# Attention and SwiGLU on one core: the feed-forward's gate and up matmuls one group ahead of their own

## The reference

```python
xn = _layernorm(x, axis=-1)
# attention: 16 heads of 8 features, 4 key/value heads, rotary embedding on q and k
q = (xn @ Wq.T + bq); k = (xn @ Wk.T + bk); v = (xn @ Wv.T + bv)
probs = softmax(q @ k * HD ** -0.5)
attn = (probs @ v) @ Wo.T + bo
# feed-forward: hidden size 384, integer weights times 1/127
h = silu(xn @ wg.T) * (xn @ wu.T)
out = x + attn + h @ wd.T
```

## Time and profile before

| what | value |
|---|---|
| runs, median (lowest to highest) | 772.57 us (772.14 to 774.59), 3 runs |
| profiled execution, its own time | 775.68 us |
| its span | 773.9 us |
| TensorE busy | 722.5 us, 93% |
| VectorE busy | 692.7 us, 90% |
| ScalarE busy | 618.1 us, 80% |
| GpSimd busy | 223.5 us, 29% |
| mean granted clock of TensorE | 0.985 of full speed |

### The profile page before, as it was taken

How to read it: one execution, slowest core, us unless ns; L and a number is a source line. 1 busy time by engine, 2 the same in 40 slices (tenths; PEclk the granted TensorE clock), 3 DMA queues, 4 the chain that set the end, 5 groups by cost and what they waited for, 6 DMA issues and landing times.

```text
span 773.9 us, 13580 instructions
## 1 busy us (share of the span) xinstructions
PE 722.5 (93%) x4856; PEld 213.2 (28%) x4856; DVE 692.7 (90%) x1284; ACT 618.1 (80%) x1267; POOL 223.5 (29%) x364
## 2 busy tenths in 40 slices
PE   3598999999999999999999999999999999999996
PEld 1222222222222222222222222222222222222352
DVE  6787999999999999999999999999999999999731
ACT  1534979888888988888888989798888889898864
POOL 3408647373830302122030303021120303021110
PEclk9787999999999999999999999999999999999999
DMA  7511123131221101011111101011111111010021
GB/s 220 140 34 32 40 76 113 33 113 33 75 71 32 32 1 54 10 31 33 32 32 32 32 22 42 1 33 32 32 32 33 32 33 32 2 32 2 2 70 40
DMA packets 29323, 34.34 MB, mean 44 GB/s; under 512 B 5545, under 2 KB 20137, under 8 KB 29129
## 3 DMA queue, kind: packets, MB, share of 16 engines
q1 hardware_dynamic: 26472, 26.23, 12.2%
q0 software_dynamic: 1920, 5.12, 2.2%
q10 hardware_dynamic: 864, 2.15, 0.8%
HBM read 23.12 MB, written 9.96 MB: 43 GB/s over the span
## 4 chain that ended last, share of the span: by engine, by line
PE 74%; DVE 15%; ACT 5%; DMA 2%; issue 2%; SPq 1%; ACTq 0%; DVEq 0%
PE acc_ps L953 29%; PE banks L867 18%; DVE mx L719 13%; PE banks L884 11%; PE banks L958 8%; ACT probs L560 5%; PE banks L972 3%; PE banks L964 2%; DMA y_all<-in_x 1%; PE banks L837 1%; PE banks L989 1%; PE banks L843 1%; DMA k_rows<-part 1%; DVE y_all L766 1%; PE banks L980 0%
## 5 line engine op out<-in xcount | busy, mean ns | idle before, releaser
L719 DVE TENSOR_REDUCE mx<-banks 128x1 f32<-128x512 f32 x1024 | 637.9, 684 | 38.1 <-PE banks L867 36.0
L560 ACT ACTIVATE probs<-banks 128x512 f32<-128x512 f32 x1024 | 549.4, 604 | 101.9 <-PE banks L884 97.8
L884 PE MATMUL banks<-qc,kc 51*128 51x512 bf16 x1024 | 305.6, 384 | 15.6 <-ACT probs L560 10.6
L867 PE MATMUL banks<-ka,qa 48*128 48x512 bf16 x1024 | 300.6, 386 | 11.1 <-DVE mx L719 6.1
L953 PE MATMUL acc_ps<-probs,v_grp 128*32 128x512 f32 x2048 | 273.4, 606 | 0.0
L867 PEld LDWEIGHTS banks<-ka,qa 48*128 48x128 bf16 x1024 | 68.7, 94 | 303.4 <-DVE mx L719 235.5
L447 POOL TENSOR_TENSOR neg_max<-row_max,nought 128x16 bf16<-128x16 f32 x31 | 6.9, 222 | 295.4 <-DVE row_max L725 295.4
L884 PEld LDWEIGHTS banks<-qc,kc 51*128 51x128 bf16 x1024 | 66.0, 94 | 55.1 <-ACT probs L560 52.3
L958 PE MATMUL banks<-xn_T,w_ffn 128*128 128x256 f32 x192 | 67.5, 433 | 0.0
L953 PEld LDWEIGHTS acc_ps<-probs,v_grp 128*32 128x32 f32 x2048 | 40.4, 108 | 81.2 <-ACT probs L560 51.1
L491 POOL TENSOR_TENSOR gated<-gu 128x256 f32<-128x256 f32 x48 | 35.2, 733 | 53.4 <-ACT gu L617 53.4
(11 more groups left out here) (86 smaller groups left out, 310.1 us busy)
## 6 DMA issues: line engine op xcount, KB each, us to landing
qa<-q_rows SPq DMA_DIRECT2D x32, 192.0 KB, 3.4
qc<-q_rows SPq DMA_DIRECT2D x64, 96.0 KB, 2.7
q_rows<-part POOLq DMA_DIRECT2D x18, 256.0 KB, 4.3
ka<-k_rows SPq DMA_DIRECT2D x32, 96.0 KB, 2.2
kc<-k_rows SPq DMA_DIRECT2D x32, 96.0 KB, 2.2
y_all<-in_x SPq DMA_DIRECT2D x4, 512.0 KB, 11.5
out<-y_all SPq DMA_DIRECT2D x8, 256.0 KB, 2.3
k_rows<-part SPq DMA_DIRECT2D x6, 192.0 KB
```

What stands on the lines that cost most here:

```text
L560: nc.scalar.activation(probs[:, s % SLOTS, j, :], banks[:, score_bank(G * s + j), :], ACT.Exp, scale=SCALE).then_inc(exp_done, 1)
L719: nc.vector.tensor_reduce(out=mx[:, h, col, k:k + 1], in_=ps, op=ALU.max, axis=AX.X).then_inc(max_done, 1)
L867: nc.tensor.matmul(ps, qa[par][rows, j // 2, t * P:(t + 1) * P], ka[par][rows, k * W:(k + 1) * W], start=True, stop=True).then_inc(a_ready, 1)
L884: nc.tensor.matmul(banks[:, score_bank(u), :], kc[par][rows, kt * P:(kt + 1) * P], qc[par][rows, h, j // 2, :], start=True, stop=True).the ...
```

## The change

The table moves the jobs, and gate and up in it now mean the chunk of group g + 1: `ffn_in` is called with g + 1, and the counts that ScalarE and TensorE wait for move by one chunk. The last group has no such jobs. Gate and up of chunk 0 are computed in the prologue, straight after the projections of batch 1, into the three banks of the first maxima: ScalarE takes them out before it normalises batch 3. GpSimd makes chunk 0's hidden values first, then adds the output bias, and only then copies v and prepares batch 0's q. VectorE's first down addition waits for the bias of its own batch and not for all four.

```diff
-JOB_AT = {1: (GATE, 0), 2: (UP, 0), 3: (GATE, 1), 4: (UP, 1), 5: (NEG_T, 1), 6: (GATE, 2), 7: (UP, 2), 8: (CTX, 0),
-          10: (DOWN, 0), 11: (DOWN, 1), 13: (NEG_T, 0), 16: (CTX, 1)}
+JOB_AT = {1: (DOWN, 0), 2: (DOWN, 1), 3: (GATE, 0), 4: (UP, 0), 5: (NEG_T, 1), 6: (GATE, 1), 7: (UP, 1), 8: (CTX, 0),
+          10: (GATE, 2), 11: (UP, 2), 13: (NEG_T, 0), 16: (CTX, 1)}
+
+FOR_NEXT = ((GATE, 0), (UP, 0), (GATE, 1), (UP, 1), (GATE, 2), (UP, 2), (NEG_T, 0))
...
     if last_group:
...
-        jobs = [JOB_AT[s]] if s in JOB_AT and JOB_AT[s] != (NEG_T, 0) else []
+        jobs = [JOB_AT[s]] if s in JOB_AT and JOB_AT[s] not in FOR_NEXT else []
...
@@ gpsimd, prologue @@
-            pool.wait_ge(ones_done, 2)
-            pool.wait_ge(v_done, 1)
-            copy_v(0, 0)
-            copy_v(1, 1)
-            pool.wait_ge(neg_step, NEG)
-            split_later(0)
+            for c in range(FC):
+                hidden(0, c)
             pool.wait_ge(xn_done, 2)
             pool.wait_ge(xn_done_act, 1)
             for b in range(B):
                 nc.gpsimd.tensor_tensor(y_all[:, b * NT:(b + 1) * NT, :], y_all[:, b * NT:(b + 1) * NT, :],
                                         bo_sb[:, :].unsqueeze(1).to_broadcast([P, NT, D]),
                                         ALU.add).then_inc(bo_added, 1)
+            pool.wait_ge(ones_done, 2)
+            pool.wait_ge(v_done, 1)
+            copy_v(0, 0)
+            copy_v(1, 1)
+            pool.wait_ge(neg_step, NEG)
+            split_later(0)
...
@@ gpsimd, groups @@
             def group(g, par):
                 split_max(g, 1)
-                for c in range(FC):
-                    hidden(g, c)
                 if g + 1 < NG:
+                    hidden(g + 1, 0)
+                    hidden(g + 1, 1)
                     split_max(g + 1, 0)
+                    hidden(g + 1, 2)
                 if g + 1 < B:
                     later(g + 1)
...
@@ scalar, prologue, between copy_later(1, 1) and the normalisation of batch 3 @@
+            for c in range(FC):
+                act.wait_ge(ffn_up, 2 * (c + 1))
+                nc.scalar.activation(th[:, c, :], first_bank(c)[:, 0:CH], ACT.Tanh, scale=0.5).then_inc(gu_done, 1)
+                nc.scalar.activation(gu[:, c, :], first_bank(c), ACT.Copy).then_inc(gu_done, 2)
...
@@ vector, add_ffn @@
-                dve.wait_ge(bo_added, B)
+                dve.wait_ge(bo_added, g // KV + 1)
...
@@ tensor, prologue @@
+            pe.wait_ge(w_done, 1)
+            for c in range(FC):
+                for n in range(2):
+                    ffn_in(0, n, c, first_bank(c)[:, n * CH:(n + 1) * CH])
             pe.wait_ge(qa_loaded[0], DMAS)
             for a in range(LEAD):
+                if a < FC:
+                    pe.wait_ge(gu_done, 3 * (a + 1))
```

More of the change, by code:

```diff
@@ L496, in hidden, with later @@
                 nc.gpsimd.tensor_tensor(hid[:, c, :], th[:, c, :], gated[:, c, :], ALU.add).then_inc(hid_done, 1)
+            for c in range(FC):
+                hidden(0, c)
+            pool.wait_ge(xn_done, 2)
+            pool.wait_ge(xn_done_act, 1)
+            for b in range(B):
+                nc.gpsimd.tensor_tensor(y_all[:, b * NT:(b + 1) * NT, :], y_all[:, b * NT:(b + 1) * NT, :],
+                                        bo_sb[:, :].unsqueeze(1).to_broadcast([P, NT, D]),
+                                        ALU.add).then_inc(bo_added, 1)
+            pool.wait_ge(ones_done, 2)
[4 more added lines that the diff above has]
+            split_later(0)
+            def later(b):
+                split_later(b)
+                for i, (_, n) in enumerate(BLOCKS):
+                    pool.dma_start(q_rows[b * KV:(b + 1) * KV, :, i, :, :].rearrange("g j d t -> (g j) d t"),
+                                   part[:, (b + 1) % 2, n, :]).then_inc(q_dma, 16)
+                pool.wait_ge(q_dma, BLOCK_DMAS * b)
+                pool.sem_inc(q_stored, 2)
             def group(g, par):
                 split_max(g, 1)
-                for c in range(FC):
-                    hidden(g, c)
                 if g + 1 < NG:
+                    hidden(g + 1, 0)
+                    hidden(g + 1, 1)
                     split_max(g + 1, 0)
+                    hidden(g + 1, 2)
                 if g + 1 < B:
@@ L609, in group @@
                         if kind == GATE:
-                            act.wait_ge(hid_done, FC * g + n + 1)
-                            act.wait_ge(ffn_up, 2 * (FC * g + n) + 1)
+                            act.wait_ge(hid_done, FC * (g + 1) + n + 1)
+                            act.wait_ge(ffn_up, 2 * (FC * (g + 1) + n) + 1)
                             nc.scalar.activation(th[:, n, :], bank(slot)[:, 0:CH], ACT.Tanh,
@@ L615, in group @@
                         if kind == UP:
-                            act.wait_ge(ffn_up, 2 * (FC * g + n) + 2)
+                            act.wait_ge(ffn_up, 2 * (FC * (g + 1) + n) + 2)
                             nc.scalar.activation(gu[:, n, CH:2 * CH], bank(slot)[:, 0:CH],
@@ L885, in scores, with ffn_in @@
                                  qc[par][rows, h, j // 2, :], start=True, stop=True).then_inc(scores_ready, 1)
+            def ffn_in(chunk, n, c, ps):
+                nc.tensor.matmul(ps, w_ffn[:, n * HID + c * P:n * HID + (c + 1) * P],
+                                 xn_T[:, chunk * CH:(chunk + 1) * CH], start=True, stop=True).then_inc(ffn_up, 1)
+            pe.wait_ge(w_done, 1)
+            for c in range(FC):
+                for n in range(2):
+                    ffn_in(0, n, c, first_bank(c)[:, n * CH:(n + 1) * CH])
             pe.wait_ge(qa_loaded[0], DMAS)
             for a in range(LEAD):
+                if a < FC:
+                    pe.wait_ge(gu_done, 3 * (a + 1))
                 if a >= FIRST_RING:
@@ L955, in weigh @@
                 last.then_inc(pv_done, 1)
-            def ffn_in(g, n, c, ps):
-                nc.tensor.matmul(ps[:, 0:CH], w_ffn[:, n * HID + c * P:n * HID + (c + 1) * P],
-                                 xn_T[:, g * CH:(g + 1) * CH], start=True, stop=True).then_inc(ffn_up, 1)
             def ffn_down_proj(g, t, ps):
@@ L997, in bank_left @@
                 elif kind == GATE:
-                    pe.wait_ge(gu_done, 3 * (FC * g + n - FC * back) + 2)
+                    pe.wait_ge(gu_done, 3 * (FC * (g + 1 - back) + n) + 2)
                 elif kind == UP:
-                    pe.wait_ge(gu_done, 3 * (FC * g + n - FC * back) + 3)
+                    pe.wait_ge(gu_done, 3 * (FC * (g + 1 - back) + n) + 3)
                 elif kind == DOWN:
@@ L1022, in take @@
                 elif kind == GATE:
-                    ffn_in(g, 0, n, ps)
+                    ffn_in(g + 1, 0, n, ps[:, 0:CH])
                 elif kind == UP:
-                    ffn_in(g, 1, n, ps)
+                    ffn_in(g + 1, 1, n, ps[:, 0:CH])
                 elif kind == DOWN:
```

## The result

The changed kernel takes 779.86 us (median of 11 runs, 776.88 to 785.07); the kernel before, measured beside it, 774.68 (11 runs, 772.14 to 776.42). The ratio is 1.0068, with a 95% interval of 1.005 to 1.0085: 5.2 us slower where 3.0 were forecast, and above the range's end of 779.0. Part of the distance is the base: the prediction counted from 772.57, the median of three runs, and eleven runs of the same kernel have their median 2.1 higher. Counted from 774.68 the same forecast is 777.7 and its range ends at 781.1; counted from 772.57 the measured change ends at 777.8. The profiled execution of the changed kernel took 777.93 with a span of 776.0, one of the shorter ones, so its span is only 2.1 above that of before, and the parts of that difference are larger than their sum.

What follows compares the result with a forecast made beforehand. TensorE or VectorE was taken to set each step's pace, with no slack on GpSimd's chain to step 5. Stalls 5.1, last group -1.7 and prologue -0.4 gave +3.0 on 772.57: 775.6 us, range 771.8 to 779.0.

Steps and rivals of the forecast that it cites:

- the base: The starting time the forecast was added to: 772.57 us, the median of the runs, 3.1 below the profiled execution.
- The three stalls: TensorE waits for GpSimd's later split at step 5 of groups 1, 2 and 3: 1.8 + 1.8 + 1.5 = 5.1 us.
- Rival A: TensorE's wait at step 5 is covered, so no stalls appear: 770.5 us; chance 0.10.
- They aren't won back: the steps after it are TensorE's: Steps behind the step 5 stalls in groups 1 to 3 recover none of the 5.1 us lost.
- The last group: Its steps lose their gate and up matmuls and get shorter: -1.7 us, bounds -0.9 and -2.3.
- The prologue: Six gate and up matmuls added before the first maxima: -0.4 us, between 1.6 earlier and 2.5 later.
- Rival B: Six matmuls keep TensorE's clock up, so the prologue gives 1.6 us: +1.8 in all, 774.4; chance 0.18.
- C: Rival: ScalarE's later normalisation delays the prologue's transposes, costing 2.5 us instead of -0.4: +5.9, 778.5; chance 0.17.
- Steps in the middle: Reordered jobs in groups before the last: each kind of step keeps its length, 0 us, bounds 0 and 0.1 a group.
- The sum: Whole kernel: stalls 5.1, last group -1.7, prologue -0.4, together +3.0 us.

Runs made afterwards that it cites:

- e5: The changed kernel run again with nothing altered; 780.01 us, ratio 1.0068 to the kernel before.
- e7: The changed kernel with the four bias additions put back behind the preparation of batch 0's q; 781.00 us, ratio 1.0073 to the kernel before.
- e8: The kernel before with three idle GpSimd additions ahead of the q preparation in groups 0, 1 and 2; 780.61 us, ratio 1.0065.
- e3: The changed kernel with GpSimd's wait for the q stores moved behind the split that TensorE waits for; 773.54 us, ratio 0.9973 to the kernel before.
- e9: The kernel before with e8's idle GpSimd additions and the wait for the stores moved behind the split; 774.56 us, ratio 1.0005.
- e6: The changed kernel with three unused TensorE matmuls before the step 5 transpose in groups 1, 2 and 3; 778.50 us, ratio 1.0043 to the kernel before.
- e12: The same kernel as e3, run once more; 771.21 us, ratio 0.9964 to the kernel before.
- e4: The kernel before with six more matmuls in the prologue whose results nobody uses; 773.33 us, ratio 0.9984.
- e11: The kernel before with six unused prologue matmuls and the wait for the stores moved behind the split; 773.94 us, ratio 0.9992.
- e2: The changed kernel with GpSimd's third product ahead of the split at step 12; 779.04 us, ratio 1.0050 to the kernel before.

## Why the prediction was wrong, point by point

- **The three stalls** are where the prediction put them, for its reason and at its size: 5.1 forecast, 5.06 in the profile, 5.9 and 5.4 in e5 and e7. e8 makes them alone, e3 and e9 take them away. Rival A (no stalls) fell.
- **The step that failed** is the sentence that ended this sum, "They aren't won back: the steps after it are TensorE's", which priced an idle TensorE at its idle time. Behind about half of these stalls TensorE runs at the lower clock. The term, put at nothing, is 3.1 us in the mean of three profiles (3.13 here, 4.61 in e5, 1.54 in e7), 3.0 by the mean clock of whole runs, and 1.5 by the medians of e5 and e6. I had the rows of the prologue, where the clock was 0.50 after an idle stretch, and did not carry them to the stalls.
- **The base** was the other term that was too small: 772.57 for a kernel whose median is 774.68 in eleven runs. Its own profiled execution, at 775.68, lay nearer to that. The base accounts for 2.1 of the 4.3 between 775.6 and 779.86, the change itself for 2.2.
- **A smaller omission** was that a chain that ends in a transfer is late by a varying amount: the wait for the stores was 4.2 to 6.0. Once the slack is gone each such delay is a stall (2.20 in group 2, 2.73 in e5), and the stalls are 5.5 in the mean of three profiles instead of 5.1. The spread of the changed kernel's runs, up to 785.07, goes with the clock instead: its two longest runs, 785.07 and 783.72, have the lowest mean clocks, 0.976 and 0.980, of 0.976 to 0.989.
- **The last group** gave 1.59 for 1.7 forecast; it is as long in e3 and e12.
- **The prologue** was forecast at -0.4 and gave 4.3 in this profile, 1.7 in the mean of the profiles, and by the medians 1.5 in e4 and nothing in e11; so its size in the median is open, and -0.4 is not refuted. The Trainium skill (TensorE: Matmul & The Clock Gate, Part 1) has the clock follow how busy TensorE has been. The clocks of 33.50 to 43.50 agree with it in direction: 0.50 to 0.54 without the six matmuls, 0.66 to 1.00 with them. I weighed against it its Part 4, that transposes don't count; the window with the same transposes and a clock of 1.00 does not bear that weight. Rival B's condition held in four of nine profiles, and there its 1.6 was too small: 3.5 against the mean of the five without. C did not happen: ScalarE's normalisation began at 33.74 and not at 34.7, and the k projection at 40.05, not 41.1.
- **Steps in the middle** kept their lengths, in all groups and apart from those behind the stalls, as forecast: down after a context job takes 2.94 (422.82 to 425.76, below).
- **The sum** with measured terms: 5.5 (mean of three profiles) + 3.1 - 1.6 - 1.7 = 5.3, against 5.2 measured. That it meets it to 0.1 is luck. The same reckoning gives -3.3 for e3 and e12 (measured -1.3 and -3.1 by the medians) and 4.9 - 1.6 - 1.7 = 1.6 for e6 (measured 2.8).

TensorE's timeline of the changed kernel, step 1 after a context job:

```profile
422.82 1.06 PE L971 MATMUL acc_ps<-probs,v_grp 128*32 128x512 f32 x8
...
425.76 1.07 PE L971 MATMUL acc_ps<-probs,v_grp 128*32 128x512 f32 x8
```

## What to carry to other kernels

Before moving work onto an engine that looks idle, follow the one chain on it that somebody waits for, and count its slack there; 2.3 us of products on an engine at 29% cost 6 to 9 us here, the difference to e3 and e12. A stall of TensorE of about 2 us can have a second price behind it, the lower clock, which here was between a quarter and a half as much again; and a wait for a store whose data is needed only later (here the next batch's q) belongs behind the work that others wait for now, which here turned a loss of 0.7% into a gain of 0.3%.

## What the runs showed of the hardware that I had not expected

A single idle stretch of 1.6 to 2.7 us, in a stream of matmuls that is otherwise busy, was followed by a lower granted clock in 6 of 13 cases, for 1.5 to 1.6 us of extra time, 3.1 in one case (e5, group 1); the idle stretch of 0.61 us that comes once in every group was followed by none; filled with three matmuls that left 0.18 to 0.36 idle it was not in 3 of 3, which is too few to be sure. Six identical GpSimd stores that in 25 of 27 cases made it wait 4.2 to 4.8 us made it wait 5.32 and 6.02 in the other two (e5 and e2). What decides whether the clock falls behind a given stall stays open.
